# First layer: value products with the values stationary in four column groups, GpSimd divides the probabilities, orders written anew

## The chip, the cores and the metric

The kernel runs on one core of a Trainium2 chip. The metric is the device time of one execution in microseconds, lower is better. The engines are TensorE (PE in the profile, its weight loads PEld), VectorE (DVE), ScalarE (ACT), GpSimd (POOL) and SyncE (SP, which here only issues DMAs). They run at once, each in the order of its own instruction queue, and wait for each other on semaphores.

## The reference, cut to what matters

A chain of four blocks works on 2 x 2048 tokens of 256 features. The change touches only the attention part of the first block:

```
q = (h @ Wq + bq) -> 16 heads of 16;  k, v = (h @ Wk + bk), (h @ Wv + bv) -> 4 heads of 16, each repeated for 4 query heads
q, k = rope(q), rope(k)
scores = q @ k.T / sqrt(16);   valid = (col <= row) & (row - col < 64)
attn = softmax(where(valid, scores, -1e9))
out  = attn @ v                      # back to 256 features
x = x + out @ Wo + bo
x = x + gelu(layernorm(x) @ Wf1 + bf1) @ Wf2 + bf2
```

Behind it come two layers of another windowed attention with a gated feed-forward part, and a last block; none of their code is changed.

## The kernel before

The first block is `layer_a`. It takes the 2048 tokens of each of the two sequences (b = 0, 1) in 16 steps of 128 tokens (`NT`). One step t does, for each b: the layer norm and its turning (`moments`, `norm`, `turn_h`), the q, k, v product (`project`), the copy of v (ACT `rope`, L488), the rotation (DVE `rope`, L633 and L636, then POOL, L421), the parts of q and k in two precisions (`parts`), their turning (`turn_qk`), the scores (`scores`, `scores2`, 8 heads each), the maxima with the mask (DVE `tops`, L657, its negative L663), the exponentials (ACT `exps`, L516, one instruction a head, 32 in a step), the turning of the probabilities (`turn_p`, `turn_p2`, evacuated by DVE and ACT), the products with the values (`values`) and the output product (`out`). The feed-forward part then takes both b together (`turn_f`, four `up`, four `gelu`, two `down`).

In `values` the turned probabilities of a head are the stationary operand (128 x 64) and the values with a column of ones (17 columns) the moving one: 32 products for each b and step, which plain f32 splits into 64 instructions. The column of ones gives the sum of each row. DVE `values` takes its reciprocal (L684) and multiplies (L685) into `o_n`; PE `turn_o` turns that (L871), ACT `turn_o` copies it to `oT` (L535), and `out` (L879) uses it. A v that the next step overwrites is first moved to `v_back` by two DMAs that SP issues (L355, L359); ACT `rope` waits for them.

Each engine's queue is written out by hand in `order`: a list of (stage, b, shift), run through once for each i, and a stage works on step t = i + shift if that exists (`turns`). So the list is the order within one steady period, and the shift says how many steps ahead or behind the stage works. Nothing else sets the order. The eight PSUM banks go round in the order of PE's list (`Ring`): a job waits until the bank's last user but one round has been drained. Plain copies by ACT need no table of functions of their own, the exponential and gelu have different ones, so each steady step has two ACT_TABLE_LOADs.

The second layer kind (`layer_b`) is named because it shows operations that the change brings into the first one: its exponentials (L1377) give the sums of rows as a second output of the activation, GpSimd multiplies the probabilities by the inverse (L1293), and its value products (L1712) use two column groups. L39 to L41 are the three lines of the helper `product3`.

## Time and profile before

| | |
|---|---|
| median of 3 runs | 2596.72 us (2589.4 to 2596.8) |
| the profiled execution | 2596.4 us, its span 2594.4 us, so 2.0 us around it |
| busy over the span | PE 95%, PEld 85%, DVE 77%, ACT 60%, POOL 49% |
| mean granted clock of TensorE | 0.966 |
| first block | about 0 to 570 us |
| one steady step of it | 285.68 us for 9 steps, 31.74 us each |

Busy time is the union of an engine's instructions. Activations overlap a little in the records: the time from the start of one to the start of the next is about 0.1 us less than its duration. The share of the whole span says little here, for the change lies in a block that is a fifth of it; the views below are of that block's steady steps.

### The profile page before, as it was taken

The numbers are of one execution on the slowest core, as the hardware profiler recorded it, in microseconds if no ns is written. First come the engines' busy times: TensorE is split into PE (matmuls) and PEld (weight loads), VectorE is DVE, ScalarE is ACT, GpSimd is POOL, SyncE is SP. The second block draws the span as 40 slices with busy tenths as digits, with TensorE's granted clock in tenths as the row PEclk, the third lists the DMA queues.
The fourth block names the chain that finished last, engine by engine and source line by source line (L and its number), as shares of the span: only waits on it lengthen the run. The fifth ranks groups of instructions, "written<-read, shape, count | busy, mean of one in ns | idle before, by whom it ended". The sixth has DMA issues, their size and how long they took to land. (4 is left out here: it accounts for less than half of the span.)

```text
span 2594.4 us, 57350 instructions
## 1 busy us (share of the span) xinstructions
PE 2452.0 (95%) x20130; PEld 2218.1 (85%) x20130; DVE 1995.1 (77%) x6034; ACT 1551.7 (60%) x3610; POOL 1283.3 (49%) x1161
## 2 busy tenths in 40 slices
PE   7999999978999999999999999999679999899997
PEld 6999999977899989988889999999668887788886
DVE  6889999858898888888888888888466556755554
ACT  4778888845777767867767778777255113431111
POOL 3233333227676566666566676665145335533332
PEclk7899999988999999999999999999789999999999
DMA  2011221121323223233332332223323013221111
GB/s 80 21 40 37 85 77 49 30 78 54 91 90 98 75 85 99 74 103 104 100 104 75 92 96 85 89 83 95 123 86 110 9 36 94 79 74 33 33 33 41
DMA packets 223618, 190.35 MB, mean 73 GB/s; under 512 B 22372, under 2 KB 205800, under 8 KB 222312
## 3 DMA queue, kind: packets, MB, share of 16 engines
q1 hardware_dynamic: 204616, 177.04, 21.9%
q10 hardware_dynamic: 18720, 9.64, 1.3%
q8 instruction: 165, 2.70, 0.4%
q14 instruction: 117, 0.96, 0.1%
HBM read 91.13 MB, written 44.04 MB: 52 GB/s over the span
## 5 line engine op out<-in xcount | busy, mean ns | idle before, releaser
L1293 POOL TENSOR_TENSOR b_sb_probs<-b_sb_probs,b_sb_r_sum 128x512 f32<-128x512 f32 x256 | 268.8, 1071 | 353.8 <-DVE b_sb_r_sum L1526 353.8
L2046 POOL TENSOR_TENSOR c_kern_lo<-c_kern,c_kern_hi 128x512 fp32r<-128x512 f32 x128 | 171.7, 1342 | 292.9 <-ACT c_kern_hi L2143 292.9
L1377 ACT ACTIVATE b_sb_probs<-b_sb_probs,b_sb_neg_top,b_sb_r_norm 128x256 f32<-128x256 f32 x512 | 301.0, 590 | 4.6 <-DVE b_sb_neg_top L1505 3.9
L2143 ACT ACTIVATE c_kern_hi<-c_kern 128x512 fp32r<-128x512 f32 x128 | 81.0, 632 | 365.7 <-DVE c_kern L2265 365.7
L39 PE MATMUL psum<-b_sb_fT_lo,b_sb_w_hi 128*128 128x256 f32 x768 | 222.8, 290 | 2.2 <-DVE b_sb_fT_lo L1564 1.4
L41 PE MATMUL psum<-b_sb_fT_hi,b_sb_w_hi 128*128 128x256 f32 x768 | 217.1, 283 | 0.0
L40 PE MATMUL psum<-b_sb_fT_hi,b_sb_w_lo 128*128 128x256 f32 x768 | 216.9, 282 | 0.0
L39 PE MATMUL psum<-c_kern_lo,c_v_hi 128*128 128x512 f32 x512 | 204.5, 399 | 0.0
L41 PE MATMUL psum<-c_kern_hi,c_v_hi 128*128 128x512 f32 x512 | 200.6, 392 | 0.0
L40 PE MATMUL psum<-c_kern_hi,c_v_lo 128*128 128x512 f32 x512 | 200.5, 392 | 0.0
L1498 DVE CUSTOM_DVE_ANT_0 b_sb_probs<-psum,b_sb_mask 128x256 f32<-128x256 f32 x512 | 194.1, 416 | 5.3 <-PE psum L1669 5.2
L2261 DVE SCALAR_TENSOR_TENSOR c_kern<-psum,c_bias 128x512 f32<-128x512 f32 x128 | 88.1, 688 | 123.5 <-PE psum L41 122.7
L39 PE MATMUL psum<-b_sb_w_lo,b_sb_hT_hi 128*128 128x512 f32 x384 | 164.2, 428 | 1.3 <-DVE b_sb_hT_lo L1447 0.6
L516 ACT ACTIVATE a_probs<-a_probs,a_neg_top 128x128 f32<-128x128 f32 x512 | 157.5, 391 | 8.4 <-DVE a_neg_top L663 7.6
L41 PE MATMUL psum<-b_sb_w_hi,b_sb_hT_hi 128*128 128x512 f32 x384 | 152.6, 397 | 0.0
L40 PE MATMUL psum<-b_sb_w_hi,b_sb_hT_lo 128*128 128x512 f32 x384 | 151.4, 394 | 0.0
L39 PEld LDWEIGHTS psum<-b_sb_fT_lo,b_sb_w_hi 128*128 128x128 f32 x768 | 145.2, 189 | 5.2 <-DVE b_sb_fT_lo L1564 1.8
L40 PEld LDWEIGHTS psum<-b_sb_fT_hi,b_sb_w_lo 128*128 128x128 f32 x768 | 145.9, 190 | 2.6
L41 PEld LDWEIGHTS psum<-b_sb_fT_hi,b_sb_w_hi 128*128 128x128 f32 x768 | 145.3, 189 | 0.0
L1690 PE MATMUL psum<-c_ident,b_sb_probs 128*128 128x128 f32 x1024 | 135.2, 274 | 5.4 <-POOL b_sb_probs L1293 3.0
L1570 DVE SCALAR_TENSOR_TENSOR b_sb_mid<-psum,b_sb_b,b_sb_gate 128x256 f32<-128x256 f32 x192 | 92.3, 481 | 56.9 <-ACT b_sb_gate L1411 55.8
L1690 PEld LDWEIGHTS psum<-c_ident,b_sb_probs 128*128 128x128 f32 x1024 | 117.3, 141 | 17.5 <-POOL b_sb_probs L1293 5.0
(307 smaller groups left out, 8773.3 us busy)
## 6 DMA issues: line engine op xcount, KB each, us to landing
b_sb_v_prev<-b_sb_v_now SPq DMA_DIRECT2D x64, 256.0 KB, 3.7
b_sb_kT_hi<-b_sb_kT_hi SPq DMA_DIRECT2D x64, 256.0 KB, 3.3
b_sb_kT_lo<-b_sb_kT_lo SPq DMA_DIRECT2D x64, 256.0 KB, 3.7
Y<-b_sb_y SPq DMA_DIRECT2D x128, 128.0 KB, 2.0
b_sb_res<-Y SPq DMA_DIRECT2D x64, 128.0 KB, 2.1
b_sb_x_f<-Y SPq DMA_DIRECT2D x128, 64.0 KB, 2.0
b_sb_res_f<-Y SPq DMA_DIRECT2D x64, 128.0 KB, 2.3
U<-c_u_out SPq DMA_DIRECT2D x16, 512.0 KB, 4.4
```

The lines of the kernel that those rows point to most:

```text
L39: pe.matmul(out, w_hi, x_lo, start=first, stop=False)
L40: pe.matmul(out, w_lo, x_hi, start=False, stop=False)
L41: return pe.matmul(out, w_hi, x_hi, start=False, stop=last)
L516: ins = act.activation(probs[b][:, h, :], probs[b][:, h, :], ACT.Exp, bias=neg_top[b][:, h:h + 1], scale=float(A_HD) ** -0.5)
L1293: pool.tensor_tensor(p, p, r_sum[b][:, 2 * m:2 * m + 2, None].broadcast_to([P, 2, 2 * P]), ALU.mult)\
L1377: ins = act.activation(probs[b][:, n, :], probs[b][:, n, :], ACT.Exp, bias=neg_top[b][:, n:n + 1], scale=r_norm[b][:, h:h + 1], accum_out= ...
L1498: ins = dve.tensor_tensor_reduce(out=probs[b][:, n, :], in0=ring.out(t, (f"s{m}", b), 512)[:, j * 256:(j + 1) * 256], in1=mask[:, min(t % ...
L1570: ring.read(t, dve.scalar_tensor_tensor(out=mid[m % 2][:], in0=ring.out(t, ("w", m), 512)[:, 256:512], scalar=b1[:, t // NT, 2 * m + 1:2 * ...
L1690: ins = pe.transpose(ring.out(t, (f"p{m}", b), 512)[:, i * P:(i + 1) * P], probs[b][:, n, half * P:(half + 1) * P], ident[:])
L2046: pool.tensor_tensor(kern_lo[i % RING][:], kern[i % RING][:], kern_hi[i % RING][:].bitcast(F32), ALU.subtract)\
L2143: act.activation(kern_hi[i % RING][:], kern[i % RING][:], ACT.Copy).then_inc(hi_ready, 1)
L2261: ring.read(dve.scalar_tensor_tensor(out=kern[i % RING][:], in0=ring.out(("scores", i), C_CHUNK), scalar=float(C_S) ** -0.5, in1=bias[:, a ...
```

## The change

Values are now stationary and the probabilities move. For each b and step there are 16 products (32 instructions): for each half of the window and each parity of the head within its group of four, the four kv heads in a row, each into 32 PSUM partitions of its own (a column group of 32). The stationary operand is 32 columns of a row `[0, v, 0]`, so that a value lands in the upper or the lower 16 partitions by the parity of the head. The output is then already turned (features by tokens): `turn_o` of PE and the DVE stage `values` go away; `Wo` is permuted on the host.

With no column of ones the sums come from `accum_out` of the 32 exponentials. DVE takes the reciprocal of 8 of them at a time (`invert`, `invert2`), and POOL multiplies the probabilities before they are turned (`scale`, `scale2`: 4 instructions of 128x512 for each b and step). In `tops` the negation of a half's maxima is placed after the first reduction of the next half. All five orders are written anew; the set-up stages are moved to the front of their queues on PE, DVE and SP and ahead of the first `turn_h` on ACT.

```diff
+        "act": [("scores2", 0, 0), ("turn_f", 0, -1), ("scores", 1, 0), ("setup_f", 0, 6), ("turn_h", 0, 1),
+                ("turn_p2", 0, 0), ("scores2", 1, 0), ("gelu", 0, -1), ("rope", 0, 1), ("turn_o", 0, 0), ("turn_h", 1, 1),
+                ("gelu", 1, -1), ("turn_p2", 1, 0), ("parts", 0, 1), ("gelu", 2, -1), ("gelu", 3, -1), ("turn_qk", 0, 1),
+                ("rope", 1, 1), ("turn_o", 1, 0), ("parts", 1, 1), ("scores", 0, 1), ("turn_qk", 1, 1)],
+        "pe": [("turn_qk", 1, 1), ("down", 1, -1), ("scores", 1, 1), ("turn_f", 0, 0), ("scores2", 1, 1), ("turn_p", 0, 1),
+               ("turn_h", 0, 2), ("turn_p2", 0, 1), ("up", 0, 0), ("values", 0, 1), ("project", 0, 2), ("turn_p", 1, 1),
+               ("up", 1, 0), ("turn_h", 1, 2), ("up", 2, 0), ("turn_p2", 1, 1), ("up", 3, 0), ("out", 0, 1),
+               ("values", 1, 1), ("turn_qk", 0, 2), ("project", 1, 2), ("setup_a", 0, 23), ("scores", 0, 2),
+               ("scores2", 0, 2), ("setup_f", 0, 2), ("out", 1, 1), ("down", 0, 0)],
+        "dve": [("moments_y", 0, -2), ("invert2", 1, 0), ("moments", 0, 2), ("finish", 0, -2), ("gelu", 0, -1),
+                ("rope", 0, 1), ("turn_p", 1, 0), ("gelu", 1, -1), ("parts", 0, 1), ("turn_h", 1, 1), ("gelu", 2, -1),
+                ("out", 0, 0), ("gelu", 3, -1), ("moments", 1, 2), ("rope", 1, 1), ("scores", 0, 1), ("out", 1, 0),
+                ("parts", 1, 1), ("moments_f", 0, 0), ("down", 0, -1), ("scores2", 0, 1), ("setup_f", 0, 1),
+                ("norm_f", 0, 0), ("down", 1, -1), ("invert", 0, 1), ("scores", 1, 1), ("invert2", 0, 1), ("norm", 0, 2),
+                ("turn_p", 0, 1), ("turn_f", 0, 0), ("scores2", 1, 1), ("invert", 1, 1), ("turn_h", 0, 2),
+                ("setup_a", 0, 7), ("norm", 1, 2)],
+        "sp": [("values", 0, 50), ("values", 1, 50), ("vshift", 0, 51), ("finish", 0, 48), ("load_r", 0, 50),
+               ("moments_y", 0, 49), ("vshift", 1, 51), ("consts", 0, 75), ("load", 0, 53), ("load", 1, 53)],
+        "pool": [("with_bias", 1, 1), ("moments", 1, 2), ("scale", 1, 1), ("scores2", 0, 1), ("moments_y", 0, -1),
+                 ("scale2", 1, 1), ("rope", 0, 2), ("parts", 0, 2), ("norm_f", 0, 0), ("moments", 0, 3), ("rope", 1, 2),
+                 ("parts", 1, 2), ("with_bias", 0, 2), ("scores2", 1, 1), ("moments_f", 0, 1), ("scale", 0, 2),
+                 ("scale2", 0, 2)],
...
+            def scaled(t, b, ms):
+                of = ms[0]
+                pool.wait_ge(r_sum_ready[of][b], t + 1)
+                for m in ms:
+                    p = probs[b][:, 4 * m:4 * m + 4, :]
+                    pool.tensor_tensor(p, p, r_sum[b][:, 4 * m:4 * m + 4, None].broadcast_to([P, 4, P]), ALU.mult)\
+                        .then_inc(p_scaled[of][b], 1)
...
             def exps(t, b, ms):
+                act.wait_ge(r_sum_ready[ms[0]][b], t)
                 for n, m in enumerate(ms):
                     act.wait_ge(top_ready[ms[0]][b], 2 * t + n + 1)
                     for j in range(4):
                         h = 4 * m + j
                         ins = act.activation(probs[b][:, h, :], probs[b][:, h, :], ACT.Exp,
-                                             bias=neg_top[b][:, h:h + 1], scale=float(A_HD) ** -0.5)
+                                             bias=neg_top[b][:, h:h + 1], scale=float(A_HD) ** -0.5,
+                                             accum_out=row_sum[b][:, h:h + 1])
...
+                m, other = ms
+                ring.wait_full(dve, t, (f"s{m}", b))
+                for j in range(4):
+                    ins = top_of(t, b, m, j)
+                ring.read(t, ins, (f"s{m}", b))
+                ring.wait_full(dve, t, (f"s{other}", b))
+                top_of(t, b, other, 0)
+                negate(t, b, m, ms[0])
...
+            def inverted(t, b, ms):
+                of = ms[0]
+                dve.wait_ge(p_ready[of][b], 2 * t + 2)
+                dve.wait_ge(p_scaled[of][b], 2 * t)
+                sums, r = (a[b][:].rearrange("p (n k j) -> p k n j", k=2, j=4)[:, of, :, :] for a in (row_sum, r_sum))
+                dve.reciprocal(r, sums).then_inc(r_sum_ready[of][b], 1)
...
             def turned_p(t, b, ms):
                 for n, m in enumerate(ms):
-                    pe.wait_ge(p_ready[ms[0]][b], 2 * t + n + 1)
+                    pe.wait_ge(p_scaled[ms[0]][b], 2 * t + n + 1)
...
+                o = ring.out(t, ("o", b), D).rearrange("p (c q) -> p c q", c=KC)
+                for half, v in ((0, v_back[b]), (1, v_now[b])):
+                    rows = slice(A_WIN * half, A_WIN * half + A_WIN)
+                    for odd in range(2):
+                        cols = slice(A_HD * (1 - odd), A_HD * (3 - odd))
+                        for kv in range(A_KV):
+                            ins = pe.matmul(o[2 * A_HD * kv:2 * A_HD * kv + 2 * A_HD, :, rows], v[:, kv, cols],
+                                            pT[b][:, A_GROUP * kv + odd:A_GROUP * kv + A_GROUP:2, rows],
+                                            start=(odd == 0), stop=(odd == 1))
+                ring.written(t, ins, ("o", b))
```

## Rows read from the trace of the kernel before

**Rows 1.** Windows: PE, PEld, DVE, ACT, POOL busy us (count), clock, DMA

```profile
139.71:425.39 285.68, 285.68 (x3368) 271.47 (x3366) 258.25 (x1180) 229.39 (x585) 89.86 (x128) 1.00 0.19 60
```

**Rows 2.** ACT by line, same stretch: xcount, busy, mean ns, idle before

```profile
L516 ACT ACTIVATE a_probs<-a_probs,a_neg_top 128x128 f32<-128x128 f32 x288 | 88.8, 391 | 3.6 <-DVE a_neg_top L663 3.2
...
L503 ACT ACTIVATE a_qT<-psum 128x512 fp32r<-128x512 f32 x36 | 19.5, 596 | 33.2 <-PE psum L809 32.8
...
L535 ACT ACTIVATE a_oT<-psum 128x256 f32<-128x256 f32 x18 | 7.0, 389 | 6.6 <-PE psum L871 6.6
```

**Rows 3.** Timeline of ACT, first block: start us, us for all of xcount

```profile
262.86 2.44 ACT L516 ACTIVATE a_probs<-a_probs,a_neg_top 128x128 f32<-128x128 f32 x8
265.20 0.58 ACT L541 ACTIVATE a_fT_hi<-psum 128x512 fp32r<-128x512 f32 x1
```

**Rows 4.** Timeline of ACT in the second layer kind, exponentials with sums

```profile
1014.28 0.60 ACT L1377 ACTIVATE b_sb_probs<-b_sb_probs,b_sb_neg_top,b_sb_r_norm 128x256 f32<-128x256 f32 x1
1014.79 0.18 ACT L1377 ACTIVATION_READ_ACCUMULATOR b_sb_probs<-b_sb_probs,b_sb_neg_top,b_sb_r_norm 128x1 f32 x1
1014.88 0.58 ACT L1377 ACTIVATE b_sb_probs<-b_sb_probs,b_sb_neg_top,b_sb_r_norm 128x256 f32<-128x256 f32 x1
```

**Rows 5.** Instructions of ACT by line, 700 to 1500 us

```profile
L1420 ACT ACTIVATE b_sb_mid_hi<-b_sb_mid 128x256 fp32r<-128x256 f32 x121 | 50.9, 420 | 33.8 <-DVEq L1575 33.8
...
L1433 ACT ACTIVATE b_sb_w_hi<-b_w_next,b_sb_gb_next 128x256 fp32r<-128x256 f32 x12 | 5.5, 513 | 0.0
```

**Rows 6.** Timeline of all engines, the chain of the rotation

```profile
50.33 0.22 ACT L488 ACTIVATE a_v_now<-psum 128x64 f32<-128x64 f32 x1 [3.42 <-PE psum L41]
...
50.59 0.49 DVE L633 TENSOR_TENSOR a_q_cos<-psum,a_rope 128x320 f32<-128x320 f32 x1 [0.38 <-ACT a_v_now L488]
...
51.68 0.86 POOL L421 TENSOR_TENSOR a_q_cos<-a_q_cos,a_q_sin 128x320 f32<-128x320 f32 x1 [8.03 <-DVEq L639]
...
52.58 0.63 ACT L496 ACTIVATE a_parts<-a_q_cos 128x512 fp32r<-128x512 f32 x1 [0.17 <-POOL a_q_cos L421]
```

**Rows 7.** Timeline of PE, first block: value products and turning of the output

```profile
266.97 0.23 PE L861 MATMUL psum<-a_v_back,a_pT 128*64 128x17 f32 x1
...
268.95 0.39 PE L39 MATMUL psum<-a_fT_lo,a_w_hi 128*128 128x256 f32 x1
...
276.56 0.38 PE L871 MATMUL psum<-a_ident,a_o_n 128*128 128x128 f32 x2
```

**Rows 8.** Timelines of PE: value products of the second layer kind; output product

```profile
1027.52 0.39 PE L1712 MATMUL psum<-b_sb_pT,b_sb_v_prev 128*64 128x128 f32 x4
1027.74 0.39 PE L1712 MATMUL psum<-b_sb_pT,b_sb_v_now 128*64 128x128 f32 x4
...
283.77 1.03 PE L879 MATMUL psum<-a_wo,a_oT 128*128 128x256 f32 x4
```

**Rows 9.** Instructions of DVE by line, nine steady steps

```profile
L685 DVE TENSOR_TENSOR a_o_n<-psum,a_r_sum 128x128 f32<-128x128 f32 x36 | 10.5, 292 | 1.2
L684 DVE RECIPROCAL a_r_sum<-psum 128x8 f32<-128x8 f32 x36 | 7.2, 199 | 0.0
```

**Rows 10.** The page's costliest groups: the same multiplication by GpSimd

```profile
L1293 POOL TENSOR_TENSOR b_sb_probs<-b_sb_probs,b_sb_r_sum 128x512 f32<-128x512 f32 x256 | 268.8, 1071 | 353.8 <-DVE b_sb_r_sum L1526 353.8
```

**Rows 11.** Timeline of all engines: a DVE instruction beside one of POOL

```profile
265.16 1.27 POOL L447 TENSOR_TENSOR a_res<-a_res_in,a_b 128x512 f32<-128x512 f32 x1 [7.78 <-DVE a_total L731]
...
265.81 0.65 DVE L663 TENSOR_SCALAR a_neg_top<-a_top 128x4 f32<-128x4 f32 x1
```

**Rows 12.** Timeline of ACT: start of the first block

```profile
9.80 0.38 ACT L481 ACTIVATE a_hT_hi<-psum 128x256 fp32r<-128x256 f32 x1 [1.45 <-PE psum L789]
...
26.01 2.19 ACT L475 ACTIVATE a_w_hi<-a_w,a_gb_f 128x1024 fp32r<-128x1024 f32 x2
...
33.94 2.45 ACT L516 ACTIVATE a_probs<-a_probs,a_neg_top 128x128 f32<-128x128 f32 x8 [2.70 <-DVE a_neg_top L663]
```

**Rows 13.** Timeline of DVE: the second load of x lands

```profile
17.80 0.43 DVE L605 BATCH_NORM_STATS2 a_stats<-a_x_in 128x6 f32<-128x256 f32 x1 [2.86 <-DMA a_x_in<-x]
```

More of the change, by code:

```diff
@@ L174, in layer_a @@
     order = {
-        "sp": [("vshift", 0, -3), ("load_r", 0, -3), ("values", 0, -3), ("load", 1, -1), ("consts", 0, -1),
-               ("values", 1, -3), ("load", 0, 0), ("finish", 0, -6), ("vshift", 1, -2), ("moments_y", 0, -5)],
-        "dve": [("gelu", 0, -3), ("moments", 0, 0), ("rope", 0, -1), ("gelu", 1, -3), ("turn_h", 1, -1), ("moments", 1, 0),
-               ("values", 1, -2), ("gelu", 2, -3), ("parts", 0, -1), ("gelu", 3, -3), ("out", 0, -2), ("rope", 1, -1),
-               ("norm", 0, 0), ("setup_a", 0, 0), ("out", 1, -2), ("moments_f", 0, -2), ("parts", 1, -1), ("setup_f", 0, -1),
-               ("finish", 0, -4), ("down", 0, -3), ("scores", 0, -1), ("norm_f", 0, -2), ("scores2", 0, -1),
-               ("turn_h", 0, 0), ("turn_p", 0, -1), ("down", 1, -3), ("scores", 1, -1), ("turn_f", 0, -2),
-               ("scores2", 1, -1), ("moments_y", 0, -3), ("values", 0, -1), ("norm", 1, 0), ("turn_p", 1, -1)],
@@ L183, in layer_a @@
-        "pe": [("turn_qk", 1, -1), ("setup_f", 0, -1), ("scores2", 0, -1), ("down", 1, -3), ("turn_h", 0, 0),
-               ("setup_a", 0, 0), ("turn_p", 0, -1), ("scores", 1, -1), ("turn_f", 0, -2), ("turn_p2", 0, -1),
-               ("scores2", 1, -1), ("values", 0, -1), ("up", 0, -2), ("turn_p", 1, -1), ("project", 0, 0), ("up", 1, -2),
-               ("turn_p2", 1, -1), ("up", 2, -2), ("turn_h", 1, 0), ("turn_o", 0, -1), ("values", 1, -1), ("up", 3, -2),
-               ("project", 1, 0), ("out", 0, -1), ("turn_o", 1, -1), ("turn_qk", 0, 0), ("out", 1, -1), ("down", 0, -2),
-               ("scores", 0, 0)],
@@ L676, in turn_p, with invert, invert2 @@
                                               ring.out(t, (f"p{m}", b), 512).rearrange("p (i q) -> p i q", i=4)), (f"p{m}", b))
[L678 to L687 removed]
+            def inverted(t, b, ms):
[4 more added lines that the diff above has]
+                dve.reciprocal(r, sums).then_inc(r_sum_ready[of][b], 1)
+            def invert(t, b):
+                inverted(t, b, halves["scores"])
+            def invert2(t, b):
+                inverted(t, b, halves["scores2"])
             def out(t, b):
@@ L752, in _ @@
             in_turns(order["dve"], NT, {"setup_a": setup_a, "setup_f": setup_f, "moments": moments, "norm": norm, "turn_h": turn_h, "rope": rope_, "parts": parts_,
-                                       "scores": scores, "scores2": scores2, "turn_p": turn_p, "values": values, "out": out,
+                                       "scores": scores, "scores2": scores2, "turn_p": turn_p, "invert": invert, "invert2": invert2, "out": out,
                                        "moments_f": moments_f, "norm_f": norm_f, "turn_f": turn_f, "gelu": gelu, "down": down,
@@ L918, in _ @@
                                       "scores2": scores2, "turn_p": turn_p, "turn_p2": turn_p2, "values": values,
[L919 removed]
+                                      "out": out, "turn_f": turn_f, "up": up, "down": down})
 def layer_b(nc, io, psum, sem, raw, early):
```

107 lines of the change are left out of this document (41 added, 66 removed).

## The prediction, made before the change was run

> **What bounds the kernel now.** I read the windows of the steady part of the first block first, because a share of the whole span averages over four blocks and only this one changes. The stretch [rows 1] holds nine steps: 288 exponentials [rows 2] at 32 a step. So a step takes 285.68 / 9 = 31.74 us. The reader is to see there that PE is busy for every one of the 285.68 us at a clock of 1.00, while DVE has 28.7 us of work a step, ACT 25.5 and POOL 10.0. PE has no gap; it sets the step. Then the lines of ACT [rows 2]: its 31.74 - 25.49 = 6.25 us of idle time a step lie mostly (33.2 us in nine steps, 3.7 a step) in front of the copy of the turned q, waiting for PE. This is room, and the question is whether the change uses more of it than PE gives back.
>
> **PE: what goes and what comes.** The value products of one b last from 266.97 to 268.95, 1.98 us, and the turning of the output 0.3 to 0.4, say 0.3 as it overlaps its neighbours [rows 7]. Both go: 2 x (1.98 + 0.3) = 4.6 us a step. New are 32 instructions for each b that move 128 columns. What such an instruction costs: the output product moves 256 columns of plain f32 in four instructions whose starts are (1.03 - 0.38) / 3 = 0.22 us apart, so 128 columns cost 0.11 us when nothing runs beside them; the value products of the second layer kind move 128 columns in two column groups, and four instructions take 0.22 us, 0.055 each [rows 8]. Two column groups therefore do run at once. Four groups at once give 32 x 0.11 / 4 = 0.87 us, only two at once 1.74, none 3.5. I take 0.87, the ends stay for the range. PE then needs 31.74 - 4.6 + 1.7 = 28.9 us a step (30.6 with two at once, 34.2 with none).
>
> **ACT: the sums of rows.** In the second layer kind an exponential with a sum is followed by an instruction of its own, a read of the accumulator of 0.18 us, which starts 0.51 us after the activation and lets the next start 0.09 us later [rows 4]. What it adds in the first block is the step I am least willing to guess, so from both sides. Eight exponentials of 128 columns there take 2.34 us from the first to the next instruction, 0.29 each, with a duration of 391 ns [rows 2, 3]. The second kind's take 0.60 each at 256 columns. The 128 more columns explain 0.1; the other 0.2 could all be the sum. But a copy of 256 columns in SBUF takes 420 ns and the same with a scale per partition 513 [rows 5], and only the second kind's exponential has such a scale. That is the missing 0.09; what remains for the sum is the 0.09 between the read and the next activation. So 32 x 0.093 = 3.0 us a step (6.0 if the read's whole duration is added, the upper end; no less than nothing, since it is one more instruction). The count of table loads stays at two, for the four blocks of exponentials still lie together in the new list. Work of ACT: 25.5 + 3.0 = 28.5.
>
> **ACT: a gap that the new order forces.** In its list `rope 1` (copy of v) is followed by `turn_o 1` and at once by `parts 1`. But DVE's rotation waits for that copy, POOL's sum for the rotation, and `parts` for POOL. With nothing in its way this chain takes from 50.33 to 52.58 = 2.25 us [rows 6]. ACT has 0.11 us of the copy and 0.39 of `turn_o` [rows 2] to fill it, so it stands still for 1.75 us in each step, whatever the others do. The old list had `turn_qk 0` and the loop's end between. Queued behind the waiting `parts 1` are the table load and the exponentials of b = 0, and with them DVE's `invert`. ACT: 28.5 + 1.75 = 30.2 us a step. This is now the longest sum.
>
> **DVE and POOL.** DVE loses four reciprocals and four multiplications, 4 x (0.20 + 0.29) = 2.0 us [rows 9], and gains four reciprocals of the same width, 0.8: 28.7 - 1.2 = 27.5. POOL gains 8 instructions of 1.07 us [rows 10]: 10.0 + 8.6 = 18.6 us. Neither is a bound by its sum. The added wait on DVE is `invert` on the exponentials; queued behind `invert2 1` are the moments and the store of y, which have room; behind `invert 0` are the maxima of b = 1, which ACT needs next. On PE `turn_p` now waits for POOL, 2 x 1.07 us after the inverse; the list puts `turn_f`, 8 exponentials and `turn_h` of ACT in between, over 4 us, so this is covered when POOL is free. The two DMAs of v carry more bytes but as many packets of a row, and wait for the same events; I cost them at nothing while `values 1` ends 2.5 us before `rope 1`. The moved negation saves some waiting on DVE, which is not the bound, up to 0.4 us a step.
>
> **What of the step is left to waiting.** I laid one period out on paper, each list in its order. Two stages come out with no room: the maxima of `scores 1` (behind PE's `out`, both `down`, `turn_qk 1` and the scores, about 11 us after ACT's `turn_qk 0`, where ACT itself takes about 12) and those of `scores2 1` (behind `invert2`, `norm`, `turn_p`, `turn_f` on DVE, 4.8 us, against 4.4 us of ACT). (These are sums of durations in the timeline: eight exponentials 3.1 and three copies 1.3 on ACT; on DVE seven reductions of 0.2, the norm 0.65, two copies of 0.65, one subtraction of 0.6 and 0.7 for the small ones.) The second alone is late by about 0.5 us. With 0.2 for the first I take 0.7 and a step of 30.9 us; from zero to the 2.3 us of the rival below.
>
> **The sum.** Steps 0 and 1 are the ramp; between the exponentials of step 2 and step 15 lie 13 periods: 13 x (30.9 - 31.74) = -10.9 us. Start of the block: the set-up of ACT, 2.19 us [rows 12] and one more instruction of as many columns, is moved ahead of the first `turn_h`, and x is loaded behind the weights. The first copy of a turned h, at 9.80 now [rows 12], then stands at about 17.8 (when a load of x that was issued behind them lands [rows 13]) plus 4 = 22 us. From there to the first exponentials it is 24.1 us now (33.94 - 9.80 [rows 12]); about 4 of them are that set-up, and I take 8 more for the bias product and the second x, which now lie in front as well (an estimate): 22 + 12 = 34, nearly no change. What PE saves while its clock is low and what the longer chain costs I set against each other. +1 us for start and end together, from -5 to +6. 2596.4 - 10.9 + 1 = 2586.5 us. The profiled execution is 0.3 us under the median of 2596.72, so no further correction.
>
> **The rivals.** (a) Only the forced gap remains: 30.2 us a step, 13 x -1.5 = -20, 2577 us. For it: PE's present list reaches no idle time at all with DVE at 90%. Against: now ACT, PE and DVE all lie above 88%.
>
> (b) The other side: GpSimd holds up DVE. A negation of 4 columns, begun at 265.81 while POOL multiplies from 265.16 to 266.43, takes 0.65 us and ends just behind POOL [rows 11], where a reciprocal of 8 columns takes 0.20 [rows 9]. POOL's new multiplications start right behind `invert 0` and `invert2 0`, that is under the first negation of `scores 1` and under `norm 0`, the two places that have no room. Price: up to 0.7 + 1.0 us, with the 0.5 above and the rest of `scores2 1` 2.2 us, a step of 32.4: 13 x 0.7 = +9, with 2 for the ramp 2607 us. It decides from 31.74 - 30.2 = 1.5 us of such waiting a step. The Trainium skill ("SBUF — State Buffer", Who interferes with whom) says that a `tensor_scalar` in a two-port mode and a GpSimd instruction lock each other out for a whole instruction. By that rule the row is no accident, and it speaks against this change.
>
> (c) The read of the accumulator costs its whole duration: 25.5 + 6.0 + 1.75 = 33.2 a step, 13 x 1.5 = +20, 2617 us. Against it: the two rows on the scale.
>
> (d) The column groups don't run four at once, so that this part doesn't do what it says: with two PE needs 30.6, less than the forecast's step, and nothing changes; with none 34.2, 13 x 2.5 = +32 and 2630 us. Against none: the pairs above.
>
> **How the numbers follow.** Forecast 0.48, (a) 0.17, (b) 0.20, (c) 0.08, (d) with none 0.07. The forecast's own range is 2580 to 2594. A measurement of this kernel can tell about 0.3%, 7.8 us, from no change: faster is below 2588.9, slower above 2604.5. Faster: (a) and two thirds of the forecast, 0.48. Same: the other third and a part of (b) with its waits half as long, 0.23. Slower: the rest of (b), (c), (d), 0.29. The range leaves out (c), (d) and the lower tail of (a): 2572 to 2614.
>
> **What would show it.** A steady step of 30.9 us by the windows, with PE no longer busy all the time (about 94%) and its clock still 1.00; a read of the accumulator 0.09 us behind each exponential; an idle time of ACT of 1.7 us in front of the copy of the parts, put down to POOL's L421 line, once a step; value products of 0.9 us for each b; negations of under 0.2 us in the two tight places. It is wrong if exponentials lie 0.48 us apart, if the value products take 3 us, if the negations and norms run into POOL's multiplications and ACT waits for them for more than 1.5 us a step, or if TensorE's clock falls in the steady part for its new gaps.

## The result: 1.1% slower, and the profile after

The changed kernel takes 2622.9 us in the median (2621.9 to 2624.0) against 2594.8 us of the kernel before, four executions of each, a ratio of 1.011 (95% interval 1.009 to 1.013): 28 us slower. The forecast was 2586.5 us with a range up to 2614, so both sign and range were missed. The profiled execution has a span of 2621.8 us.

A step of the steady part now takes 33.77 us, against 31.77 before (six periods in each, from the second to the eighth start of POOL's second sum of the residual). 13 periods of 2.00 us more are 26 of the 28 us. The start is as forecast: the first exponentials begin at 33.76 us, where they stood at 33.94 [rows 12]. So the whole question lies in the steady step. The windows of six steps (columns as in [rows 1]):

```profile
123.40:326.02 202.62, 182.21 (x1841) 164.94 (x1844) 187.50 (x763) 170.30 (x583) 111.42 (x134) 0.99 0.13 39
```

Divided by six: PE 30.37 us a step, DVE 31.25, ACT 28.38, POOL 18.57. PE, which had no gap in [rows 1], now stands still for 3.4 us. ACT and POOL have the sums forecast (28.5 and 18.6); DVE was forecast at 27.5 and is the fullest engine. Its lines in the same stretch, those that changed first (xcount, busy us, mean ns, idle before):

```profile
L666 DVE TENSOR_TENSOR a_parts<-a_q_cos,a_parts 128x512 fp32r<-128x512 f32 (+1 forms) x25 | 21.3, 888 | 0.0
...
L635 DVE TENSOR_SCALAR a_xn<-a_x_in,a_mv,a_rstd 128x256 f32<-128x256 f32 x12 | 13.5, 1128 | 0.0
L782 DVE TENSOR_SCALAR a_y_out<-a_total,a_mv_y,a_rstd_y 128x256 f32<-128x256 f32 x12 | 13.0, 1123 | 0.0
L680 DVE TENSOR_SCALAR a_neg_top<-a_top 128x4 f32<-128x4 f32 x48 | 10.9, 228 | 0.8
```

The same three in the kernel before, over the nine steps of [rows 1]:

```profile
L647 DVE TENSOR_TENSOR a_parts<-a_q_cos,a_parts 128x512 fp32r<-128x512 f32 (+1 forms) x36 | 15.9, 484 | 0.0
...
L616 DVE TENSOR_SCALAR a_xn<-a_x_in,a_mv,a_rstd 128x256 f32<-128x256 f32 x18 | 7.5, 419 | 0.0
...
L748 DVE TENSOR_SCALAR a_y_out<-a_total,a_mv_y,a_rstd_y 128x256 f32<-128x256 f32 x18 | 6.6, 410 | 4.1 <-DMA Y<-a_y_out 4.1
```

There xn took 419 ns, y_out 410 and `parts` 484 in the mean. Now the first two take 1.12 us and the third 0.89, though their shapes are the same; that is 2 x 0.71 + 2 x 0.71 + 4 x 0.40 = 4.4 us a step. The reciprocal (200 ns, 199 in [rows 9]) and the moments of the second norm (413 ns, 418 before) have not changed; in this kernel neither of them lies beside a multiplication of POOL. What lies beside the long ones, in the timeline of all engines:

```profile
257.22 1.27 POOL L462 TENSOR_TENSOR a_res<-a_res_in,a_b 128x512 f32<-128x512 f32 x1
257.83 2.48 DVE L666 TENSOR_TENSOR a_parts<-a_q_cos,a_parts 128x512 fp32r<-128x512 f32 x2
258.57 1.60 POOL L464 TENSOR_TENSOR a_res<-a_res,a_x 128x512 f32<-128x512 f32 x1
...
276.52 2.21 POOL L441 TENSOR_TENSOR a_probs<-a_probs,a_r_sum 128x512 f32<-128x512 f32 x2 [1.04 <-DVE a_r_sum L715]
276.71 1.13 DVE L635 TENSOR_SCALAR a_xn<-a_x_in,a_mv,a_rstd 128x256 f32<-128x256 f32 x1
...
285.91 2.09 POOL L441 TENSOR_TENSOR a_probs<-a_probs,a_r_sum 128x512 f32<-128x512 f32 x2
285.98 2.17 DVE L782 TENSOR_SCALAR a_y_out<-a_total,a_mv_y,a_rstd_y 128x256 f32<-128x256 f32 x2
```

Each long instruction of DVE lies beside a 128x512 instruction of POOL and ends near the end of one (a record of x2 is two instructions in a row). It is the pattern of [rows 11], mostly at other places than those I priced. The Trainium skill ("SBUF — State Buffer", Who interferes with whom) says that an instruction of VectorE with two inputs in SBUF contends with GpSimd's reads too, not only the two-port modes; `parts` is such an instruction and agrees (2.48 us for a pair beside POOL, 0.88 for the pair of b = 1). I had used only the rule's other half.

ACT shows the forced gap (the end of the first line), its wait for the negated maxima and the price of the sums:

```profile
L512 ACT ACTIVATE a_parts<-a_q_cos 128x512 fp32r<-128x512 f32 x12 | 7.6, 634 | 10.5 <-POOL a_q_cos L422 10.5
...
L533 ACT ACTIVATE a_probs<-a_probs,a_neg_top 128x128 f32<-128x128 f32 x192 | 74.3, 390 | 7.3 <-DVE a_neg_top L680 7.2
...
267.19 0.40 ACT L533 ACTIVATE a_probs<-a_probs,a_neg_top 128x128 f32<-128x128 f32 x1
267.50 0.19 ACT L533 ACTIVATION_READ_ACCUMULATOR a_probs<-a_probs,a_neg_top 128x1 f32 x1
267.59 0.39 ACT L533 ACTIVATE a_probs<-a_probs,a_neg_top 128x128 f32<-128x128 f32 x1
```

10.5 us in six steps are 1.75 a step, and the exponentials' starts lie 0.40 and 0.39 apart where eight of them took 2.34 us [rows 3]. On PE the four column groups do run at once: the 32 value products of one b start within 0.8 us and take 1.08 in all:

```profile
258.50 0.64 PE L897 MATMUL psum<-a_pT,a_v_back 128*32 128x128 f32 x16
258.96 0.62 PE L897 MATMUL psum<-a_pT,a_v_now 128*32 128x128 f32 x16
...
L875 PE MATMUL psum<-a_ident,a_probs 128*128 128x128 f32 x192 | 26.8, 277 | 5.8 <-DVE a_mid_lo L756 5.7
...
L823 PE MATMUL psum<-a_ident,a_xn 128*128 128x128 f32 x24 | 4.9, 286 | 8.5 <-DVE a_xn L635 8.5
```

The last line says where PE's largest wait comes from: xn, the instruction that GpSimd stretches, 8.5 us in six steps. The line above it says that the turning of the probabilities waits for DVE and not for POOL, so the longer way from the exponentials over the inverse and the multiplication is not what PE waits for here.

### The profile page after: what moved, and what is told of

It is laid out like the page before. It is cut to its first block and busy times, and to the rows that moved or that the text cites. A ratio compares the mean times of both kernels' runs of the same rounds, so it can differ in the third digit from the quotient of the medians.

```text
span 2621.8 us, 55875 instructions
## 1 busy us (share of the span) xinstructions
PE 2426.3 (93%) x19042; PEld 2174.6 (83%) x19042; DVE 2029.2 (77%) x5970; ACT 1599.0 (61%) x4122; POOL 1418.2 (54%) x1289
## 5 line engine op out<-in xcount | busy, mean ns | idle before, releaser
L533 ACT ACTIVATE a_probs<-a_probs,a_neg_top 128x128 f32<-128x128 f32 x512 | 198.1, 390 | 15.8 <-DVE a_neg_top L680 15.6
L441 POOL TENSOR_TENSOR a_probs<-a_probs,a_r_sum 128x512 f32<-128x512 f32 x128 | 134.5, 1072 | 108.0 <-DVE a_r_sum L715 108.0
```

Source lines behind the costliest of these rows:

```text
L441: pool.tensor_tensor(p, p, r_sum[b][:, 4 * m:4 * m + 4, None].broadcast_to([P, 4, P]), ALU.mult)\
L533: ins = act.activation(probs[b][:, h, :], probs[b][:, h, :], ACT.Exp, bias=neg_top[b][:, h:h + 1], scale=float(A_HD) ** -0.5, accum_out=ro ...
```

## The experiments

Three theories stood at first. Contention: GpSimd's multiplications and sums lengthen DVE's instructions, and DVE sets the step. Rival: ScalarE's longer work (row sums and gap) sets it. Second rival: the longer chain from the exponentials to the turned probabilities sets it. "Step" is the mean of steady periods, busy times are us a step. Most versions ran once and are compared with the kernel before on the same chip; the kernel before itself took 2587.7 to 2602.0 us in 19 executions, so a difference of a few us between two single executions says nothing. The steps, read from the traces, are steadier (31.80 and 31.81 us in two executions of one version).

### Is it the load of GpSimd? In both kernels

The kernel before, with eight spare multiplications of the same shape for each step:

```diff
+                if b == 1:
...
+                    for n in range(8):
...
+                        pool.tensor_tensor(spare, ones[:, None, :].broadcast_to([P, 4, P]), mask[:, 1:2, :].broadcast_to([P, 4, P]), ALU.mult)\
...
```

> The kernel before, with 8 more GpSimd multiplications of 128x512 in each step of the first block, from constants into a tile that nobody reads, right behind `scores2` of b = 1; nobody waits for them. Contention theory: VectorE's instructions that lie beside them (negations L663, norms L615 and L616) take 0.5 to 1 us instead of 0.17 and 0.41, VectorE's busy time in a step rises from 28.7 to 30 or more, and the step from 31.74 to 32 to 33 us. Theories of ScalarE's sum or of the chain: nothing of either is added here, the step stays at 31.7 within 0.2.

Measured: 2609.7 us against 2595.7, step 32.96 instead of 31.77, DVE 30.3 instead of 28.7.

```profile
107.34:305.08 197.74, 194.73 (x2254) 183.62 (x2252) 181.67 (x787) 154.69 (x392) 122.31 (x135) 0.99 0.14 45
...
L624 DVE TENSOR_SCALAR a_xn<-a_x_in,a_mv,a_rstd 128x256 f32<-128x256 f32 x12 | 11.2, 934 | 0.0
```

Work that nobody waits for, on an engine that was two thirds idle, costs 14 us: xn goes from 419 to 934 ns. (One of the six periods took 33.96 us at a granted clock of 0.95; the other five, at 1.00, 32.76 in the mean.) Then the changed kernel with its multiplication cut to one column for each head (the probabilities stay unscaled but for that column):

```diff
-                    pool.tensor_tensor(p, p, r_sum[b][:, 4 * m:4 * m + 4, None].broadcast_to([P, 4, P]), ALU.mult)\
+                    pool.tensor_tensor(p[:, :, 0:1], p[:, :, 0:1], r_sum[b][:, 4 * m:4 * m + 4, None], ALU.mult)\
```

> The changed kernel; GpSimd multiplies 1 of the 128 columns of each head only (128x4 instead of 128x512), so most probabilities stay undivided; order, waits and count of instructions stay. Takes the contention of the new multiplications and 2 x 0.9 us of the chain away, but not the overlap of `parts` with the residual's sums. Contention theory: L634, L635, L680 and L782 go back to about 0.41, 0.41, 0.17 and 0.41 us, VectorE's busy time falls by about 3 us a step, the step to 31.5 to 32.5 us. ScalarE's sum: step stays above 33. (The chain's theory also expects a fall, of 1 to 2 us, with VectorE's times unchanged.)

Measured: 2590.6 us against 2595.7, step 31.35. The windows, and xn again at its old length:

```profile
120.69:308.81 188.12, 178.80 (x1840) 163.67 (x1844) 164.69 (x763) 168.76 (x583) 71.19 (x134) 1.00 0.14 42
...
L635 DVE TENSOR_SCALAR a_xn<-a_x_in,a_mv,a_rstd 128x256 f32<-128x256 f32 x12 | 4.9, 407 | 0.0
```

DVE's 164.69 / 6 = 27.45 us is the 27.5 of the forecast; `parts` keeps its 894 ns, as POOL's residual sums stay beside it. The step is a little below the 31.5 to 32.5 us that contention expected. But this edit shortens two things, the load and the chain exponential, reciprocal, multiplication, turn. So the narrow multiplications first, and behind them as many spare full ones whose result nobody reads:

```diff
+                for m in ms:
...
+                    pool.tensor_tensor(spare, ones[:, None, :].broadcast_to([P, 4, P]), mask[:, 1:2, :].broadcast_to([P, 4, P]), ALU.mult)\
...
```

> The changed kernel; at each of the four places of a step GpSimd first does the two narrow multiplications (128x4, most probabilities stay undivided), which releases the turning, and only then two full ones of 128x512 from constants into a tile that nobody reads. So GpSimd's load is as in the changed kernel and a little more, while the chain from the exponentials to the turning is 1.8 us shorter. Contention theory (GpSimd's load holds up VectorE): the step stays at 33.4 to 34.4 us, with L634, L635 and L782 at about 1.1 us. Theory of the chain: the step falls to 31.4 to 32 us as with the narrow multiplications alone.

Measured: 2609.4 us against 2600.7, step 32.93, DVE 30.2. Both theories missed: contention expected 33.4 us or more with xn at about 1.1 us, the chain 32 or less. Of the 2.4 us between 33.77 and 31.35, 1.6 come back with the load alone. The other 0.8 are not shown to be the chain's, since the spare multiplications start later and hold DVE less: xn takes 893 ns instead of 1128, y_out 906 instead of 1123, and PE's wait for xn falls from 8.5 to 4.1 us in six steps, which is 0.7 us a step:

```profile
L832 PE MATMUL psum<-a_ident,a_xn 128*128 128x128 f32 x24 | 4.9, 286 | 4.1 <-DVE a_xn L644 4.1
```

### Is it ScalarE?

The exponentials without their sums (the sums are a constant 1, so nothing is divided by them):

```diff
-                                             accum_out=row_sum[b][:, h:h + 1])
```

> The changed kernel without `accum_out` of the 32 exponentials; the sums are a constant 1, so the probabilities are not divided by their sum. ScalarE loses 32 x 0.093 = 3.0 us of work a step. If ScalarE's sum sets the step: 33.76 falls by 2 to 3 us. Contention theory with VectorE as the bound: the step falls by under 0.7 us and ScalarE's idle time grows by 2.3 us or more.

Measured: 2616.1 us against 2595.7; ACT falls from 28.4 to 25.9 us, and the step stays at 33.78, as DVE's 31.2 does. The 7 us gained lie outside the steady steps: the first instruction of the second block on PE starts at 588.92 us instead of 591.64, and the rest lies in code that both kernels share, where single executions differ by as much. ScalarE doesn't set the changed kernel's step. Next, the forced gap of ACT: on PE `project 1` goes ahead of `turn_qk 0`, on ACT `rope 1` likewise, and on DVE `turn_h 1` ahead of `parts 0`.

```diff
-               ("values", 1, 1), ("turn_qk", 0, 2), ("project", 1, 2), ("setup_a", 0, 23), ("scores", 0, 2),
+               ("values", 1, 1), ("project", 1, 2), ("turn_qk", 0, 2), ("setup_a", 0, 23), ("scores", 0, 2),
```

> The changed kernel with three pairs of neighbours swapped, so that the copy of v of b = 1 no longer stands two instructions ahead of the copy of the parts: on PE `project 1` ahead of `turn_qk 0`, on ScalarE `rope 1` ahead of `turn_qk 0`, on VectorE `turn_h 1` ahead of `parts 0`. Theory that the forced gap of ScalarE is on the path: its idle time of 1.75 us in front of the parts falls under 0.8 and the step by 0.8 to 1.5 us. Contention theory (VectorE is full): the idle time moves to another place of ScalarE, the step falls by under 0.4.

Measured: 2629.9 us against 2600.7, step 34.6. This mean has periods of 34.6 and 36.5 us in it in which the granted clock was 0.95; at 1.00 most periods take 33.96 us, 0.2 more than in the changed kernel. The gap falls from 1.75 to 1.3 us, and other waits take its place (three steps at clock 1.00):

```profile
L504 ACT ACTIVATE a_v_now<-psum 128x64 f32<-128x64 f32 x6 | 1.3, 222 | 4.7 <-DMA a_v_back<-a_v_now 4.7
...
L855 PE MATMUL psum<-a_kT,a_qT 64*128 64x128 f32 x192 | 12.7, 276 | 3.1 <-ACT a_kT L524 3.1
```

The copy of v, done earlier, meets the DMA that still reads the old one (1.6 us a step, 0.4 before this edit), and PE gets its q and k later (1.0). So shortening the gap in this way gains nothing; what the gap alone costs isn't shown.

### Moving DVE's work out from under GpSimd

First POOL's sums of the residual, the neighbours of `parts 0`, made to wait until `parts 0` has passed:

```diff
+                pool.wait_ge(parts_ready[0], min(t + 3, NT))
                 pool.tensor_tensor(res[:], res_in[:], b2[:, None, :].broadcast_to([P, BATCH, D]), ALU.add).then_inc(r_own, 1)
```

> The changed kernel; GpSimd starts its two sums for the residual (L462, L464, 1.27 and 1.60 us) only once VectorE's two `parts` instructions of b = 0 are done. Contention theory (VectorE and GpSimd lock each other out, and VectorE is the bound of the step): `parts` of b = 0 falls from 2.48 us to about 0.9, L464 from 1.60 to 1.27, a step from 33.76 to 32.2 to 32.8 us, the time by 13 to 22 us under the changed kernel's. Theory that ScalarE's own sum plus the forced gap of 1.75 us sets the step: `parts` shortens as well, but the step stays at 33.76 within 0.3. Theory of the longer chain (exponentials, inverse, multiplication, turning): no change either.

Measured: 2626.2 us against 2595.7, step 33.8. The contention theory had expected 32.2 to 32.8 us and the others no change, so taken alone this run goes against it. `parts` is back at 484 ns as expected, but the edit makes a wait of its own:

```profile
L729 DVE TENSOR_TENSOR a_x<-psum,a_xh_bo 128x256 f32<-128x256 f32 x12 | 5.1, 425 | 11.8 <-POOL a_res L465 11.6 <-issue 0.3
```

11.6 / 6 = 1.9 us a step, since `out 0` waits for the sums that now come later. So 1.6 us of stretching were traded for 1.9 us of waiting, and the run doesn't decide between the theories. Then the scalings: `finish` behind `parts 1`, `norm 0` behind `norm_f`, `norm 1` ahead of `invert 1`; nothing is left out and no instruction added (SP's store of y moves with `finish`):

```diff
-        "dve": [("moments_y", 0, -2), ("invert2", 1, 0), ("moments", 0, 2), ("finish", 0, -2), ("gelu", 0, -1),
+        "dve": [("moments_y", 0, -2), ("invert2", 1, 0), ("moments", 0, 2), ("gelu", 0, -1),
...
-                ("parts", 1, 1), ("moments_f", 0, 0), ("down", 0, -1), ("scores2", 0, 1), ("setup_f", 0, 1),
-                ("norm_f", 0, 0), ("down", 1, -1), ("invert", 0, 1), ("scores", 1, 1), ("invert2", 0, 1), ("norm", 0, 2),
-                ("turn_p", 0, 1), ("turn_f", 0, 0), ("scores2", 1, 1), ("invert", 1, 1), ("turn_h", 0, 2),
-                ("setup_a", 0, 7), ("norm", 1, 2)],
+                ("parts", 1, 1), ("finish", 0, -2), ("moments_f", 0, 0), ("down", 0, -1), ("scores2", 0, 1), ("setup_f", 0, 1),
+                ("norm_f", 0, 0), ("norm", 0, 2), ("down", 1, -1), ("invert", 0, 1), ("scores", 1, 1), ("invert2", 0, 1),
+                ("turn_p", 0, 1), ("turn_f", 0, 0), ("scores2", 1, 1), ("norm", 1, 2), ("invert", 1, 1), ("turn_h", 0, 2),
+                ("setup_a", 0, 7)],
```

> The changed kernel with three of VectorE's stages moved to where GpSimd stands still: `finish` behind `parts 1`, `norm 0` behind `norm_f`, `norm 1` ahead of `invert 1` (and the store of y behind it on SyncE). Nothing is left out. Contention theory: L634, L635 and L782 fall from 0.74 to 1.13 us to about 0.41 to 0.5, VectorE's busy time by 2.5 to 3 us a step, the step to 32 to 32.8 us, 13 to 22 us under the changed kernel's time. If only the multiplications' own time in the chain counts: the step stays within 0.3 of 33.76.

> The kernel of e7_scalars_moved_off_gpsimd, timed in rounds. Contention theory: 2597 us as in its one look, a ratio to before of 0.998 to 1.002, so that the three stages moved take back the whole loss of the change but bring no gain. Rival, that the one look was a lucky order: 2605 us or more, ratio above 1.003.

Measured: 2596.9 us in one execution; in ten, 2594.2 us against 2594.1, ratio 1.000 (0.999 to 1.001). The step is 31.80 us, below the 32 to 32.8 expected. Moving three stages in one list gives back the whole loss:

```profile
120.72:311.50 190.78, 177.93 (x1837) 163.18 (x1836) 172.09 (x763) 168.03 (x583) 109.15 (x134) 1.00 0.14 41
...
L635 DVE TENSOR_SCALAR a_xn<-a_x_in,a_mv,a_rstd 128x256 f32<-128x256 f32 x12 | 4.9, 408 | 0.0
L776 DVE TENSOR_SCALAR a_var_y<-a_mv_y 128x2 f32<-128x2 f32 x6 | 5.3, 878 | 0.2
...
L875 PE MATMUL psum<-a_ident,a_probs 128*128 128x128 f32 x192 | 27.0, 278 | 9.1 <-POOL a_probs L441 9.1
```

POOL does nearly the same work (109 us, 111 before), but the three stages of DVE no longer lie beside it, and DVE falls from 31.25 to 28.7 us a step. That is the plainest evidence for contention. The move is not clean: a small scaling of 128x2 (L776) now lies beside a multiplication and takes 878 ns, where it took 170. And PE now does wait for POOL's multiplied probabilities, 9.1 us in six steps. In the same kernel the sums of the residual were then moved ahead on POOL, behind `moments_f`, and given a second buffer so that they need not wait for y:

```diff
-                    ring.wait_last_drained(pool, t, ("y", b))
+                    if t > 1:
+                        ring.wait_drained(pool, t - 2, ("y", b))
...
-                pool.tensor_tensor(res[:], res[:], x1[:], ALU.add).then_inc(res_ready, 1)
+                pool.tensor_tensor(res_at(t), res_at(t), x1[:], ALU.add).then_inc(res_ready, 1)
```

> The three stages moved off GpSimd's scaling as in e7_scalars_moved_off_gpsimd, and in addition the residual sums write into two buffers in turn and their squares' sums, so that GpSimd does them one stage of the order earlier and not beside `parts 0`. Theory, contention: in e7 the one instruction still stretched was `parts` (895 ns mean, 2.48 us for the pair of b = 0 beside the residual sums against 0.88 us for b = 1). With that gone DVE falls from 28.7 to about 27 us a step, and the step from 31.8 to between 30.6 and 31.5 us: 2575 to 2592 us in all, below the kernel before. Rival, ScalarE's gap: the step of e7 is already set by ACT's 28.0 us busy, 1.75 us gap and its waits, and then DVE's 1.6 us turn into waiting, step 31.7 and 2597 us. Second rival: the sums land beside another instruction of VectorE and stretch that one: `parts` falls, another group rises by as much, step unchanged.

Measured: 2587.9 us against 2594.1, ratio 0.998 (0.997 to 0.999), step 31.37, DVE 27.9. Both the theory and its second rival are half right: `parts` falls from 895 to 510 ns (1.5 us a step), and the negations rise from 261 to 343 ns (0.7), because the sums now lie beside those. This kernel beats both others, the kernel before by only 0.2%. With the gap's edit of above added to these two, the gain is lost again:

> The changed kernel with the moves of VectorE's three stages, the three swaps for the copy of v, and GpSimd's two sums for the residual placed behind `moments_f`, one step earlier, for which the residual alternates between two tiles. Nothing is left out. Contention theory: VectorE's `parts` of b = 0 falls from 2.48 to 0.9 us, busy VectorE to 27 to 28.5 us a step, the step to 30.4 to 31.5 us and the time below the kernel before, 2575 to 2592 us. If the step stays above 32.5, another wait takes over that no theory here names.

Measured: 2612.1 us against 2600.7, step 33.4, so above the 32.5 from which the expectation asked for another wait. DVE stays at 27.7 us a step, so it isn't contention; over the six steps ACT waits 1.6 us a step for the DMA of v and PE 1.35 for q, as above. Part of it is the clock again: it is 0.91 or 0.95 in three of these six periods; two others, at 1.00, take 32.03 and 32.05 us, 0.8 more than the 31.26 of most periods without this edit.

### What do the row sums cost, then?

The forecast had put ScalarE's 3.0 us a step into ACT's idle time. In the kernel before, with the sums written where nobody reads them:

```diff
                         ins = act.activation(probs[b][:, h, :], probs[b][:, h, :], ACT.Exp,
-                                             bias=neg_top[b][:, h:h + 1], scale=float(A_HD) ** -0.5)
+                                             bias=neg_top[b][:, h:h + 1], scale=float(A_HD) ** -0.5,
+                                             accum_out=wqkv[:, b, h:h + 1])
```

> The kernel before, with the sums of the rows that the change asks ScalarE for, written to a buffer that nobody reads. Theory of the prediction: ScalarE's idle time covers them; ACT's busy time rises from 25.5 by 3.0 to 28.5 us a step, the step stays at 31.77 us, and the time within 3 us of before. Rival, that the exponentials' latency is on the path of PE and DVE (values and divisions wait for the last one of a group): the step rises by up to 0.19 us for each of four groups, 0.4 to 0.8 us, 5 to 10 us in all.

Measured: 2622.3 us against 2594.1, most steps 33.63 us, with ACT's work up from 25.5 to 28.2 us. Both sides of the expectation were wrong: the sums alone cost the kernel before as much as the whole change did. Two of the 13 steady periods take 36.3 us instead. In each of them the granted clock fell, here one of them and the period behind it:

```profile
239.71:276.01 36.30, 35.12 (x377) 33.24 (x374) 28.87 (x132) 28.36 (x99) 10.01 (x14) 0.91 0.11 33
276.01:309.65 33.64, 32.44 (x377) 30.31 (x374) 28.70 (x132) 28.23 (x99) 9.87 (x15) 1.00 0.26 98
```

From about 242 to 249 us it is 0.5 (the level of 1.2 GHz), with PE busy all the time at half speed; in the 8 us ahead of that PE had stood still twice for 0.6 us, waiting for the exponentials. Each such fall costs 2.7 us here. In the kernel before, whose PE has no gap, the clock stays at 1.00 through all steady periods. Then only those of b = 0:

```diff
+                        if b == 0:
+                            ins = act.activation(probs[b][:, h, :], probs[b][:, h, :], ACT.Exp,
+                                                 bias=neg_top[b][:, h:h + 1], scale=float(A_HD) ** -0.5,
+                                                 accum_out=wqkv[:, b, h:h + 1])
```

> The kernel before with the unread row sums of b = 0 alone (16 of 32 reads). In e12_before_with_row_sums 32 reads, 3.0 us of ACT, raised the step from 31.77 to 33.63, 0.62 of each us. Theory, a loop through ACT in which every exponential stands (no idle row between the table load ahead of the exponentials and the end of the gelus): it is paid in proportion from the first one, 0.9 us, step 32.7. Rival, a slack that is used up first (3.0 us less 1.1 us of slack): half the reads, 1.5 us, cost 0.4 us, step 32.2.

Measured: 2623.6 us against 2591.2, step 33.24. Neither of the two was right. The 16 reads of b = 0 cost 33.24 - 31.77 = 1.47 us, which is their whole length (16 x 0.093 = 1.49); the 16 of b = 1 add 0.39. The trace shows where (six steps):

```profile
L503 ACT ACTIVATE a_qT<-psum 128x512 fp32r<-128x512 f32 x24 | 13.0, 596 | 22.2 <-PE psum L814 21.9
...
L846 PE MATMUL psum<-a_ident,a_probs 128*128 128x128 f32 x195 | 28.0, 276 | 7.1 <-ACT a_probs L517 7.1
```

PE, which had no wait at all, now waits 1.2 us a step for the exponentials of b = 0, and ACT's idle time in front of L503 is 22.2 / 6 = 3.7 us a step as in [rows 2]. This idle time was not used up by the added work; it lies behind PE's wait and moves with it. (Of this kernel's 32 us, 27.4 lie in the first block, by the start of the second one at 592.60 us instead of 565.20: 13 x 1.47 = 19, 3 for one period of 36.3 us at a clock of 0.91, 3 ahead of the steady steps, the rest behind them. The other 5 lie in code that both kernels share and are within the spread of single executions.)

Last, the sums taken out, by the edit shown above for the changed kernel, of the three versions in which contention is smaller: the one with the moved stages, that with the second buffer, that with the narrow multiplication.

> e7_scalars_moved_off_gpsimd without the sums of the rows: the exponentials have no accumulator and the rows' sum is a constant 1, so the probabilities aren't normalised; all other instructions stand. Theory that ScalarE is the next bound once the contention is gone: ACT's busy time falls by some 2.5 us a step (as in e3_no_row_sums) and the step falls with it, from 31.8 to 30.8 or less, 2585 us or less. Rival, that DVE and its waits still bound it: step 31.6 to 31.9, and only what e3_no_row_sums also lost outside the steady part, some 7 us: about 2590 us.

> e9_residual_alternates (31.37 us a step, 2588 us) without the row sums (rows' sum a constant 1, so the probabilities aren't normalised). Theory, ScalarE's late exponentials: with the contention gone as well the row sums cost 0.6 us a step or more, as between e10 and e11 (31.81 to 31.18): step 30.3 to 30.8, 2570 to 2580 us. Rival, another wait (PE's for the probabilities) is next: step 31.1 to 31.4.

> The changed kernel with both added loads taken out: the multiplication of e4_narrow_multiplication (128x4) and no row sums (rows' sum a constant 1, so the probabilities aren't normalised), while the values stationary, the outputs born turned and the new orders stay. Theory, several near-equal bounds: e4 stands at 31.35 us with ScalarE at 28.1; e3 alone gained nothing a step, e11 0.6 us, and the row sums put into the kernel before cost it 1.9 us. So here the step falls to between 29.8 and 30.8 us, towards PE's 29.6 us busy, and the time to 2560 to 2580 us. Rival, that the new orders' own waits (the 1.75 us of ACT for q_cos, PE for the probabilities) bind whatever the loads: step 31.1 or more, 2585 us or more.

Measured: 2578.8 us against 2594.1 and step 31.18 without the sums, 31.80 with them; 2589.3 against 2591.2 and step 31.37, with them 31.37; 2581.9 against 2591.2 and step 30.69, with them 31.35. So the sums cost 0.6 us, nothing and 0.7 us a step. In the first one the step lies between the two theories (30.8 or less, 31.6 or more), in the third it fell as the theory had it, with the time 2 us above its range. In the second one the first theory fell and its rival came, and the windows of both (eight steps) show why, that without the sums first, and PE's wait with them:

```profile
130.90:381.89 250.99, 238.63 (x2450) 217.47 (x2449) 223.38 (x1017) 206.77 (x521) 142.57 (x178) 1.00 0.19 62
```

```profile
132.98:383.97 250.99, 238.77 (x2450) 217.62 (x2450) 223.20 (x1017) 225.52 (x776) 142.55 (x177) 1.00 0.19 63
...
L881 PE MATMUL psum<-a_ident,a_probs 128*128 128x128 f32 x256 | 37.7, 280 | 11.8 <-POOL a_probs L446 11.8
```

PE's 238.8 us and its wait of 11.8 us (11.9 without the sums) for the multiplied probabilities are the whole stretch, with the sums and without. So there PE's work and its wait for POOL make the step; POOL's multiplications in turn wait for DVE's inverse (26.8 us in the eight steps). Whether another order of POOL's list would shorten this was not tried.

The steps together, with what each kernel has of the two added loads:

| us a step | neither | row sums | multiplication | both |
|---|---|---|---|---|
| before | 31.77 | 33.63 | 32.96 (spare) | not run |
| changed | 30.69 | 31.35 | 33.78 | 33.77 |

Without its two loads the change would gain 1.1 us a step (the 32.96 has the period with the lower clock in it; 32.76 without). The row sums cost 1.9 us in the old order and 0 to 0.7 in the new one; the multiplication costs 2.4 to 3.1 us in the new one. The costs don't add: in the changed kernel the multiplication hides the row sums.

## Why the prediction was wrong

**PE's saving: right in kind, too large.** Four column groups run at once, 1.08 us for each b where 0.87 was taken. Without either load PE is busy for 29.7 us a step, not 28.9; the value products explain 0.4 of the difference, the rest is open.

**ACT's sum: right; its cover: wrong.** 0.093 us for each sum, 28.4 us against 28.5, no table load more, and rival (c) was rightly held unlikely: of the read's 0.19 us about half lies beside the end of its activation and half beside the start of the next. (Taking the sums out lowers ACT's busy time by 2.5 us a step, not by 3.0; why was not looked into.) But "room" of 6.25 us was read from ACT's idle time. The runs on the kernel before showed that the 16 exponentials of b = 0 stand on PE's path there, at full price, while 3.7 us of idle time stay untouched. That this error didn't show in the result is chance: the new order and the larger error hide it.

**ACT's gap: right to the hundredth (1.75), but ACT's sum is not the step.** With the contention mostly gone ACT's 28.2 + 1.75 = 29.9 us stand in a step of 31.37. The orders that shortened the gap lost time to other waits. Rival (a), a step of 30.2 us, did not come in any version that keeps both loads.

**DVE: the step that failed.** "28.7 - 1.2 = 27.5" and, behind it, "Neither is a bound by its sum": the sum kept every duration as it was in the old order. In the changed kernel DVE has 31.25 us, because the new list puts its scalings and `parts` beside POOL's multiplications and sums, and the step is 33.77 us where 30.9 was forecast: 13 x 2.00 = +26 us instead of -10.9. With the narrow multiplication DVE has 27.45, close to the forecast, but by two shifts that cancel: `parts` 4 x 0.41 = 1.6 us more, negations (177 ns, 270 before) and xh (409, 671 before) 8 x 0.09 + 2 x 0.26 = 1.3 less, since POOL's old work no longer lies beside these. That the sum came out is luck. The full multiplication adds 3.8 us to it, with no instruction of DVE changed.

**Rival (b) named the mechanism and was mis-sized.** Its price was 1.7 us at two places, the first negation and `norm 0`. The first negation and xn of `norm 0` did pay, 0.58 us instead of 0.17 and 1.13 instead of 0.42, together 1.1. The other negations stay at 0.17 to 0.25 us; `norm` of both b, the two scalings of `finish` and the pair of `parts 0` paid, because the new lists put them beside POOL. I looked only at stages without room, when every instruction of DVE that can be held up beside POOL's 18.6 us was to be counted: xn and y_out 2 x 0.7 each, `parts` 1.6. It gave 32.4 us a step and 2607 where 33.77 and 2622.9 came. Of its sign, more than 1.5 us a step of such waiting, ACT shows only 1.2 (7.2 us in six steps for the negations); PE waits 1.4 for xn and 0.8 for `parts`, which the sign left out. Given this, 0.20 was too little: [rows 11] showed the pattern, and the change nearly doubles POOL's work.

**The waits** of 0.7 us a step on top of 30.2 were too few for any version that keeps both loads: 3.6 us in the changed kernel, 1.2 in the best one (31.37 - 30.2). There PE waits 1.5 us a step for POOL's multiplication. "over 4 us, so this is covered when POOL is free" was the sentence on it; it held only while DVE was later still.

**Start: right by luck.** The first exponentials differ by 0.2 us, as forecast, but the first copy of a turned h stands at 19.35 us, not at 22, and from there it takes 14.4 us, not 12: two misses that cancel.

**Clock: nearly right.** The steady part's mean is 0.99. It fell to 0.95 in two of the 13 periods, which was one of the signs of being wrong; these took 33.73 and 33.98 us, so it cost 0.3 us at most, since PE has idle time there.

## What to carry to other kernels

An engine's idle time is room only if its work isn't on the way of another's wait; the cheapest test is to add the work alone to the old kernel and see what it costs. In these runs work moved to GpSimd was paid by VectorE wherever a scaling in SBUF or an instruction with two SBUF inputs lay beside one of its 128x512 instructions: list what stands beside each new GpSimd instruction in the new order, and put reductions, reciprocals and reads of PSUM there. Three stages moved in a list were worth as much as the whole change. Look at the granted clock of each period before you read a mean of periods: a few falls of it hid here in means that looked like waits.

## What the runs showed of the hardware

Beside a 128x512 instruction of GpSimd, a `tensor_scalar` of 128x256 on VectorE takes 1.12 us instead of 0.41, one of 128x2 0.88 instead of 0.17, and a pair of 128x512 `tensor_tensor` with both inputs in SBUF 2.48 instead of 0.88. Other instructions stay as they were beside the same multiplications: two copies of 128x512 from PSUM (1.27 us) and the masked maxima (0.28) in the changed kernel, two batch moments (0.74) with the stages moved, reciprocals of 8 columns (0.19) with the second buffer. GpSimd is held up far less: its whole busy time changed from 109 us to 111 in six steps between the kernel with the stages moved and the changed one, its second sum of the residual alone from 1.28 to 1.60 us. An accumulator read behind an activation shows 0.19 us and moves the next start by 0.093. With row sums in the kernel before, whose PE then waits 1.2 us a step, the granted clock fell to 0.5 for some 7 us in two of 13 periods, at 2.7 us each; other versions whose PE waits as long or longer show no such fall in their steady periods, so what sets it off is open.
